# One attention and mixture-of-experts block: scores in one run, a native fp32 weighted sum, and a re-ordered opening

## The chip, the cores and the metric

The kernel runs on one core of one Trainium2 chip. The metric is the device time of one execution in microseconds (us), of which 532.69 is the median of three runs before the change. TensorE (PE in the views) does matmuls and transposes, VectorE (DVE), ScalarE (ACT) and GpSimd (POOL) do element work, and SyncE (SP) issues most of the DMAs. Each engine runs its own instructions in the order of the program and waits on semaphores for the others.

## The reference, cut to what matters

```python
# x: (32, 64, 256); a first layer, then a second one that the change does not touch
xn = ln(x, g_norm)
q = (xn @ Wq).reshape(b, n, 16, 64)          # 16 heads of 64
k, v = split(xn @ Wkv)                       # one key and one value for all heads
k, v = [null_k; k], [null_v; v]              # a null position in front (per batch row)
q, k = l2norm(q) * q_scale, l2norm(k) * k_scale
sim = q @ k.T * 8 + rel_pos_bias(...)        # position network: pos -> ln, silu -> ln, silu -> 16 heads
attn = softmax(where(causal & mask, sim, -big))
z = ln((attn @ v) @ Wout, g_out)
x = x + (((z Wq'.T)(z Wk'.T).T * scale * decay) @ (z Wv'.T)) @ Wo'.T * out_scale
x = x + ffn(moe(x))                          # router, 8 experts, shared expert, dense layer
```

## The kernel before

The 2048 rows are 16 tiles of 128 rows (NT = 16), and a tile is two sequences of 64 rows, b = 0 in the partitions 0 to 63 and b = 1 in 64 to 127. The first layer is a software pipeline over an index i from -2 to 18. In one body(i) the engines work on several tiles at once: the projection of tile i+1, the scores of tile i, the weighted sum of tile i-1, the output projection and second norm of tile i-2, and the retrieval of tile i-3. `live(off)` says whether tile i+off exists. The bodies -2 to 3 and the last ones are written out with extra steps between them, and 4 to 13 are a loop. The order of each engine is the order in which its block is written; nothing plans it.

What a body does, as far as the change touches it:

- Tile i+1: ScalarE makes `xn` from the row statistics, TensorE transposes it into bank 0, ScalarE and VectorE split it into an upper and a lower part (`xnT_h`, `xnT_l`, type fp32r), and TensorE multiplies by the projection in three banks, 384 columns each (`split_passes`, lines 317 to 319: three passes of the split product). An extra matmul with `nvhl` (line 1417) subtracts the null value from v. Squares, sums and a power on GpSimd give `rn`, with which VectorE writes `qn`.
- The value of a tile is laid out as a block diagonal matrix in `vblk_h`, `vblk_l` (four copies on ScalarE, four subtractions on VectorE).
- Tile i: 32 small matmuls (64 rows by 64 columns of the array, 65 columns moved, line 1375) give the scores. The two heads of the last pair share bank 3; TensorE waits for the first (`sc7`) and does the second behind the retrieval's matmuls (line 1388). VectorE adds the bias (`biasm`) in three pieces to `sim`, takes the maximum; GpSimd subtracts it, ScalarE takes the exponential `pe`, VectorE sums (`den`) and inverts (`rden`), and GpSimd writes `pr`.
- Tile i-1: TensorE transposes `pr` (line 1400), ScalarE and VectorE split it into `pT_h` and `pT_l`, and two times three fp32r matmuls over 128 rows, 512 columns each, give the weighted sum in banks 6 and 7. ScalarE and VectorE split that into `oT_h` and `oT_l`.
- Tile i-2: 16 matmuls with `oT_h` and 8 with `oT_l` (line 1339), then the statistics of the second norm.
- The statistics of the rows of x are taken tile by tile: `layer_norm_stats` on VectorE between the sums of the squares, and four small operations on GpSimd behind the `rn` (lines 564 to 570).

The opening (bodies -2 to 0) has beside that the position network (`position_stats`, `hidden_transpose`, `hidden_project`, `silu`), which ends in `relT`, a store to DRAM and two loads back as `bias`; the folding of the retrieval's weights (`fold_qk`, `fold_vo`); and the splitting of the weights, `wout_lower` among them. GpSimd makes the constants (`constants`, `late_constants`) before the first `rn`.

Of the kernel before, what the change touches and what calls it, by code (L numbers as in the profile page):

```python
# [3 lines left out]
F32 = mybir.dt.float32  # L4
# [4 lines left out]
ALU = mybir.AluOpType  # L9
# [38 lines left out]
def adaln_attention_ffn(nc, a, out):  # L48
    ctx = ExitStack()
    with ctx:  # L50
# [39 lines left out]
        with ExitStack() as first:  # L90
# [11 lines left out]
            nvhl = s1('nvhl', [2, DH], F32R)  # L102
            nvf = s1('nvf', [2, DH])
# [8 lines left out]
            ve1 = s1('ve1', [P, 1])  # L112
            ve2 = s1('ve2', [P, 1])
            rs1 = s1('rs1', [P, 1])
            rs2 = s1('rs2', [P, 1])
            nb1 = s1('nb1', [P, 1])
            nb2 = s1('nb2', [P, 1])
            nm1 = s1('nm1', [P, 1])
            nm2 = s1('nm2', [P, 1])
            fixed = s1('fixed', [P, 2])  # L120
            xn = s1('xn', [P, D])
# [10 lines left out]
            vblk_h = s1('vblk_h', [P, 2, 2, P], F32R)  # L132
            vblk_l = s1('vblk_l', [P, 2, 2, P], F32R)
# [13 lines left out]
            with ExitStack() as early2:  # L147
# [11 lines left out]
                nkB, nullb, nvr = nulls[:, 0:DH], nulls[:, DH:DH + H], nulls[0:2, DH + H:2 * DH + H]  # L159
                nksq = s2('nksq', [P, DH])  # L160
                mask_u = s2('mask_u', [P, NT, S], U8)
                zeros = s2('zeros', [P, 2, 2, P])
            pT_h = s1('pT_h', [P, HP, P], F32R)
            pT_l = s1('pT_l', [P, HP, P], F32R)
# [64 lines left out]
        for n in '''ld_x0 ld_x1 ld_x2 ld_rows ld_qkv ld_q2 ld_out ld_att ld_mlp ld_cols ld_mask ld_late st_rel ld_bias ld_u ld_f st_out  # L229
                    pc vc p_const p_tables p_ln    v_zero v_null  v_ln v_hn  # L230
                    v_rawqkv v_lower v_fold   v_decay  v_lin
                    a_sil a_qkvh a_wouth  a_decay   a_tables  
                    t_hT t_mlp t_fold    unit_h unit
                    mv1 ln1_ve ln1_rs ln1_nb xn xnT xnT_h xnT_l qkv sq ss ss_c rn qn kn2 v_h
                    kT_t kh sc7 vblk qT_t qT sim_t biasm sim mx simc pe den rden pr
                    pT_t pT_h pT_l av_t oT_h oT_l wo_t mv2 ln2_ve ln2_rs ln2_nb zn
# [26 lines left out]
        def score_place(r, c):  # L263
            return (bank[3], r * NK) if c == LAST_PAIR else (bank[2 - r], c * NK)

        def score_part(t, m):
            return t[:, 2 * LAST_PAIR:H, :] if m == 2 else t[:, 1 - m:2 * LAST_PAIR:2, :]

        def score_bank(m):
            n = (LAST_PAIR, LAST_PAIR, 2)[m]  # L270
            return bank[1 + m][:, 0:n * NK].rearrange('p (h k) -> p h k', k=NK)
# [43 lines left out]

        def split_passes(e, dst, stat, mov, start, stop, **kw):
# [12 lines left out]
        def _(e):  # L329
# [10 lines left out]
            e.dma_start(nulls[:, :], a['nulls'].to_broadcast([P, 2 * DH + H])).then_inc(sems['ld_cols'], 16)  # L340
# [14 lines left out]
            for b in range(2):  # L355
                e.dma_start(bias[b * S:(b + 1) * S, :, 0:S], rel_dram.ap().rearrange('h i j -> i h j')).then_inc(sems['ld_bias'], 16)
# [61 lines left out]
        def _(e):  # L418
# [21 lines left out]
            def constants():  # L440
                e.memset(zeros[:, :, :, :], 0.0).then_inc(sems['pc'], 1)
                e.wait_ge(sems['pc'], upto('pc'))
# [14 lines left out]
            def late_constants():  # L457
                e.wait_ge(sems['ld_mask'], 16 * 1)
                e.tensor_scalar(mneg[:, :, 0:S], mask_u[:, :, :], -1.0, BIG, ALU.add, ALU.mult).then_inc(sems['pc'], 1)
                e.wait_ge(sems['pc'], upto('pc'))  # L460
                e.memset(zrow[:, :], 0.0).then_inc(sems['pc'], 1)
# [8 lines left out]
                e.wait_ge(sems['pc'], upto('pc'))  # L470
                for n in range(WORD):
# [11 lines left out]

            def after_norm0():
                constants()
                position_norm(1)
# [3 lines left out]
                late_constants()  # L490

            def after_first_projection():
                e.wait_ge(sems['rn'], NB3)
                e.wait_ge(sems['ln1_nb'], 2)
                e.wait_ge(sems['v_null'], 2)
                e.tensor_copy(kh[:, :, S], colsc[:, NKK:NKK + 1].to_broadcast([P, 2])).then_inc(sems['p_tables'], 1)
                e.wait_ge(sems['p_tables'], upto('p_tables'))
                e.tensor_copy(bias[:, :, S:NK], nullb.rearrange('p (h o) -> p h o', o=1)).then_inc(sems['pc'], 1)
                e.wait_ge(sems['pc'], upto('pc'))

            def first_bias():
                e.wait_ge(sems['ld_bias'], 16 * 2)
# [9 lines left out]
            def mask_decay():  # L512
                e.wait_ge(sems['a_decay'], 3)
# [5 lines left out]
            def after_second_scores():  # L519
                e.wait_ge(sems['v_lower'], 1)  # L520

            def mask_bias(i):
                e.wait_ge(sems['sim'], due(NB3 * i))
# [7 lines left out]
            def body(i, par, live, part):  # L531
                if live(0):
                    e.wait_ge(sems['rn'], due(NB3 * (i + 1)))
                    e.wait_ge(sems['ln1_nb'], due(i + 2 if live(1) else NT))
# [27 lines left out]
                if live(2):  # L562
                    e.wait_ge(sems['mv1'], due(2 * (i + 3)))
                    e.tensor_tensor(nm1[:, :], mv[:, 0, 0:1], fixed[:, 1:2], ALU.mult)
                    e.tensor_tensor(ve1[:, :], mv[:, 0, 1:2], fixed[:, 0:1], ALU.add).then_inc(sems['ln1_ve'], 1)
                    e.wait_ge(sems['ln1_ve'], due(i + 3))
                    e.wait_ge(sems['xn'], due(i + 2))
                    e.tensor_tensor(rs1[:, :], ve1[:, :], half[:, 0:1], ALU.pow).then_inc(sems['ln1_rs'], 1)
                    e.wait_ge(sems['ln1_rs'], due(i + 3))
# [1134 lines left out]
```

## Time and profile before

| what | value |
|---|---|
| time, median of 3 runs (lowest, highest) | 532.69 us (531.86, 539.52) |
| span of the profiled execution | 532.0 us |
| TensorE busy | 468.7 us (88%) |
| VectorE, ScalarE, GpSimd busy | 359.7, 274.7, 284.7 us |
| mean granted clock of TensorE | 0.958 |

The profiled execution's own time is its span, 532.0 us, which is 0.7 us under the median; the views below are all of that execution. The span is read in three stretches: the opening to about 60 us, the tiles of the first layer to about 295 us, and the second layer behind it. Busy shares are means over all three.

### The profile page before, as it was taken

Reading aid. Unit: us, or ns where it says so; the run is one execution under the profiler, and the core shown is the slowest. Engines: PE = TensorE matmul, PEld = TensorE weight load, DVE = VectorE, ACT = ScalarE, POOL = GpSimd, SP = SyncE. Lnnn points to the kernel's source line nnn. Section 1 sums busy time; section 2 is a strip of 40 time slices with the busy share of each in tenths; the row PEclk is TensorE's granted clock in tenths of the full one; section 3 lists DMA queues with packets and bytes.
Section 4 is the critical chain, followed back from the end, with each engine's and each line's share of the span. In section 5 each row is a group of like instructions: output and inputs, shape, how many; then the busy total and the mean of one; then the engine's idle time right before and its main releaser. Section 6 shows DMA issues by size and latency. Waiting matters only on the chain.

```text
span 532.0 us, 11898 instructions
## 1 busy us (share of the span) xinstructions
PE 468.7 (88%) x3961; PEld 418.7 (79%) x3961; DVE 359.7 (68%) x879; ACT 274.7 (52%) x574; POOL 284.7 (54%) x343
## 2 busy tenths in 40 slices
PE   3946889999999999999999896499989489999997
PEld 1735777898999988898888785398989359898986
DVE  4784888888889888898766475757664524444522
ACT  3426666576667666566652422246565234453442
POOL 3738778897987979797830777400000633425100
PEclk9966999999999999999998998989999879999999
DMA  8370103709082641000010323265752312213011
GB/s 263 90 192 1 31 1 111 257 26 343 0 292 72 208 157 30 0 30 1 1 31 2 99 100 108 82 206 185 235 169 100 89 33 57 80 41 96 25 41 39
DMA packets 51616, 52.17 MB, mean 98 GB/s; under 512 B 6645, under 2 KB 49015, under 8 KB 51577
## 3 DMA queue, kind: packets, MB, share of 16 engines
q1 hardware_dynamic: 47956, 42.98, 25.5%
q0 software_dynamic: 3072, 8.39, 5.0%
q8 instruction: 23, 0.38, 0.3%
q10 hardware_dynamic: 548, 0.28, 0.2%
q14 instruction: 17, 0.13, 0.1%
HBM read 22.03 MB, written 29.62 MB: 97 GB/s over the span
## 4 chain that ended last, share of the span: by engine, by line
PE 59%; issue 8%; POOL 8%; ACT 5%; DMA 3%; DVE 3%; SPq 1%; DVEq 0%; ACTq 0%; POOLq 0%
PE bank L317 10%; PE bank L318 9%; PE bank L319 9%; POOL slot_x L579 6%; PE bank L322 5%; PE bank L323 5%; PE bank L1375 3%; PE bank L1655 3%; PE bank L1400 2%; PE bank L1339 2%; PE bank L1443 2%; ACT qT L666 2%; PE bank L1351 1%; PE bank L1388 1%; DMA slot_y<-yb 1%
## 5 line engine op out<-in xcount | busy, mean ns | idle before, releaser
L588 POOL DMA_INDIRECT yg<-slot_y,yrow x32 | 34.2, 1068 | 120.8 <-DMA slot_y<-yb 76.3
L561 POOL TENSOR_TENSOR rn<-sc,half 128x6 f32<-128x6 f32 (+1 forms) x48 | 60.6, 1277 | 7.9 <-DVE sc L1023 6.9
L1256 DVE TENSOR_TENSOR hl<-hw,hh 128x512 fp32r<-128x512 f32 x32 | 22.2, 693 | 57.1 <-ACT hw L837 57.1
L835 ACT ACTIVATE hh<-bank,late 128x512 fp32r<-128x512 f32 x32 | 22.0, 688 | 53.5 <-PE bank L1655 41.9
L317 PE MATMUL bank<-wqkv_h,xnT_h 128*128 128x384 f32 x96 | 39.1, 408 | 6.8 <-DVE sim L1004 6.8
L556 POOL TENSOR_TENSOR sim<-sim,mx 128x1040 f32<-128x1040 f32 x16 | 31.3, 1955 | 23.0 <-DVE mx L1007 23.0
L695 ACT ACTIVATE sq<-bank 128x384 f32<-128x384 f32 (+1 forms) x48 | 22.8, 475 | 40.3 <-PE bank L319 24.7
L524 POOL TENSOR_TENSOR biasm<-bias,mneg 128x1040 f32<-128x1040 f32 x16 | 35.7, 2229 | 3.7 <-DMA bias<-rel_scratch 3.7
L579 POOL DMA_INDIRECT slot_x<-xs,posi x32 | 31.4, 980 | 11.2 <-issue 9.4
L542 POOL TENSOR_TENSOR pr<-pe,rden 128x1024 f32<-128x1024 f32 x16 | 30.4, 1903 | 9.2 <-DVE rden L1044 4.5
L322 PE MATMUL bank<-wout_h,oT_h 128*128 128x256 f32 x128 | 33.6, 296 | 1.9 <-DVE oT_l L1038 1.9
L318 PE MATMUL bank<-wqkv_l,xnT_h 128*128 128x384 f32 x96 | 34.5, 359 | 0.0
L319 PE MATMUL bank<-wqkv_h,xnT_l 128*128 128x384 f32 x96 | 34.3, 358 | 0.0
L322 PE MATMUL bank<-w_h,hh 128*128 128x256 f32 x128 | 32.5, 287 | 0.0
L323 PE MATMUL bank<-wout_l,oT_h 128*128 128x256 f32 x128 | 32.4, 289 | 0.0
L323 PE MATMUL bank<-w_l,hh 128*128 128x256 f32 x128 | 32.0, 283 | 0.0
L1020 DVE TENSOR_REDUCE ss<-sq 128x6 f32<-128x384 f32 (+1 forms) x48 | 25.2, 526 | 7.5 <-ACT sq L695 7.4
L1004 DVE TENSOR_TENSOR sim<-bank,biasm 128x455 f32<-128x455 f32 (+1 forms) x48 | 21.9, 513 | 11.2 <-PE bank L1375 11.2
L674 ACT ACTIVATE zn<-bank,nb,rs 128x256 f32<-128x256 f32 x16 | 9.1, 566 | 39.4 <-POOL nb L551 39.4
L317 PE MATMUL bank<-wu_h,bxT_h 128*128 x80 | 25.1, 314 | 2.5 <-DVE bxT_l L1205 2.5
L322 PEld LDWEIGHTS bank<-wout_h,oT_h 128*128 128x128 f32 x128 | 24.9, 195 | 2.5 <-issue 1.4
L317 PEld LDWEIGHTS bank<-wqkv_h,xnT_h 128*128 128x128 f32 x96 | 19.5, 204 | 9.1 <-issue 8.3
(317 smaller groups left out, 1604.8 us busy)
## 6 DMA issues: line engine op xcount, KB each, us to landing
slot_x<-zrow SPq DMA_DIRECT2D x4, 4352.0 KB, 14.4
xq<-slot_x SPq DMA_DIRECT2D x40, 128.0 KB, 2.1
slot_y<-yb SPq DMA_DIRECT2D x20, 256.0 KB, 2.4
fstage<-in_f_W SPq DMA_DIRECT2D x4, 512.0 KB, 4.5
out<-p_all SPq DMA_DIRECT2D x8, 256.0 KB, 2.1
xs<-in_x SPq DMA_DIRECT2D x1, 1536.0 KB, 9.5
raw_out<-in_c_Wout SPq DMA_DIRECT2D x1, 1024.0 KB, 7.8
stage<-in_m_wgate SPq DMA_DIRECT2D x8, 128.0 KB, 2.1
```

Of the source, the lines that this page charges most:

```text
L317: e.matmul(dst, stat[0], mov[0], start=start, stop=False, **kw)
L318: e.matmul(dst, stat[0], mov[1], start=False, stop=False, **kw)
L319: return e.matmul(dst, stat[1], mov[0], start=False, stop=stop, **kw)
L322: e.matmul(dst, stationary, moving[0], start=start, stop=False, **kw)
L323: e.matmul(dst, stationary, moving[1], start=False, stop=False, **kw)
L524: e.tensor_tensor(biasm[:, :, :], bias[:, :, :], (mneg[:, i:i + 1, :] if isinstance(i, int) else mneg[:, bass.ds(i, 1), :]).to_broadcast([ ...
L542: e.tensor_tensor(pr[:, :].rearrange('p (h k) -> p h k', h=H), pe[:, :, 0:S], rden[:, :].rearrange('p (h o) -> p h o', o=1).to_broadcast([ ...
L556: e.tensor_tensor(sim[:, :, :], sim[:, :, :], mx[:, :].rearrange('p (h o) -> p h o', o=1).to_broadcast([P, H, NK]), ALU.subtract).then_inc ...
L561: e.tensor_tensor(rn[:, lo:hi], sc[:, lo:hi], half[:, lo:hi], ALU.pow).then_inc(sems['rn'], 1)
L579: e.indirect_dma_start(out=xdram.ap()[:, :], out_offset=bass.IndirectOffsetOnAxis(ap=posi[:, t, r:r + 1], axis=0), in_=xs[:, t, :], in_off ...
L588: e.indirect_dma_start(out=yg[:, g % 2, r, t, :], out_offset=None, in_=ydram.ap()[:, :], in_offset=bass.IndirectOffsetOnAxis(ap=yrow[:, g ...
L1020: e.reduce_sum(ss[:, lo:hi], sq[:, lo:hi, :], AX_X).then_inc(sems['ss'], 1)
```

## The change

- **Scores.** The two sequences of a tile take opposite row halves of the array: for b = 1 the heads of a pair are exchanged (`r ^ b`), in the scores, in the null bias and in the loads of `bias`. The last pair goes to banks 3 and 5, so the wait `sc7` goes, and the 32 matmuls stand in one run. The bias is added in four pieces instead of three.
- **Weighted sum.** `pT_h`, `pT_l`, `vblk_h`, `vblk_l` and `nvhl` go. There is one fp32 copy `pT` and two values `v_own` and `v_other` (three subtractions of `nvB` on VectorE, at the end of the body), and the sum is four fp32 matmuls over 64 rows and 64 columns of the array, 512 columns moved.
- **Order in a body.** On TensorE the eight matmuls with `oT_l` stand behind the transposes of `qn`. On VectorE `qn` stands ahead of `den` and `rden`. On ScalarE `kn2` stands ahead of `oT_h` and `pe`.
- **Row statistics.** They are taken in groups of tiles, X_GROUPS = (0), (1), (2, 3), (4 to 7), (8 to 11), (12 to 15): `row_stats` at the end of VectorE's bodies -1 to 3 and `norm_rows` behind GpSimd's.
- **Opening.** `hidden_project(0)` stands ahead of the transposes of `xn`, `position_scale(0)` ahead of the wait for the small tables; ScalarE loads its function tables early by two one-column activations (`warm`); `late_constants` is cut in three, of which two stand behind the first projection's `rn`; `wout_lower` moves from body 0 to behind body -1, `fold_vo` from ahead of the scores' bias to behind the maximum.

```diff
+        X_GROUPS = ((0, 1), (1, 2), (2, 4), (4, 8), (8, 12), (12, NT))
+        SCORES = ((2 * LAST_PAIR, H - 1, 3), (2 * LAST_PAIR + 1, H, 5), (1, 2 * LAST_PAIR, 1), (0, 2 * LAST_PAIR, 2))
...
             def after_first_projection():
                 e.wait_ge(sems['rn'], NB3)
-                e.wait_ge(sems['ln1_nb'], 2)
                 e.wait_ge(sems['v_null'], 2)
                 e.tensor_copy(kh[:, :, S], colsc[:, NKK:NKK + 1].to_broadcast([P, 2])).then_inc(sems['p_tables'], 1)
                 e.wait_ge(sems['p_tables'], upto('p_tables'))
+                norm_rows(1)
                 e.tensor_copy(bias[:, :, S:NK], nullb.rearrange('p (h o) -> p h o', o=1)).then_inc(sems['pc'], 1)
                 e.wait_ge(sems['pc'], upto('pc'))
+                row_constants()
+                late_constants()
...
+            def norm_rows(n):
+                t0, t1 = X_GROUPS[n]
+                e.wait_ge(sems['mvx'], 2 * (n + 1))
+                e.tensor_tensor(nmx[:, t0:t1], mvx[:, t0:t1, 0], fixed[:, 1:2].to_broadcast([P, t1 - t0]), ALU.mult)
...
+                e.tensor_tensor(rsx[:, t0:t1], vex[:, t0:t1], half[:, 0:t1 - t0], ALU.pow).then_inc(sems['ln1_rs'], 1)
...
             def after_first_scores():
+                norm_rows(2)
...
             def after_second_scores():
+                norm_rows(3)
                 e.wait_ge(sems['v_lower'], 1)
...
-                    e.wait_ge(sems['ln1_nb'], due(i + 2))
+                    e.wait_ge(sems['ln1_nb'], x_groups_for(i + 1 if isinstance(i, int) else i))
...
+            def row_stats(n):
+                t0, t1 = X_GROUPS[n]
+                e.wait_ge(sems[('ld_x0', 'ld_x0', 'ld_x1', 'ld_x2', 'ld_x2', 'ld_x2')[n]], 16 * 1)
+                for t in range(t0, t1):
+                    last = e.bn_stats(stx[:, t - t0, :], xs[:, t, :])
...
+                if live(1):
+                    e.wait_ge(sems['av_t'], due(2 * i))
...
+                    e.tensor_tensor(v_own[:, 1 - par, :], bank[NB3][:, values], nvB[:, :], ALU.subtract)
...
+                if isinstance(i, int) and FIRST_I < i < FIRST_I + len(X_GROUPS):
+                    row_stats(i - FIRST_I)
...
-                    head = slice(r * DH, (r + 1) * DH)
                     for b in range(2):
+                        head = slice((r ^ b) * DH, ((r ^ b) + 1) * DH)
                         last = e.matmul(dst[b * S:(b + 1) * S, lo:lo + NK], qT[head, c, b * S:(b + 1) * S], kh[head, b, :], start=True, stop=True)
...
-                        last = split_passes(e, bank[6 + b][:, :], (vblk_h[:, 1 - par, b, :], vblk_l[:, 1 - par, b, :]), (pT_h[:, :, b * S:(b + 1) * S], pT_l[:, :, b * S:(b + 1) * S]), True, True)
...
+                    for q in range(2):
+                        rows = slice(q * S, (q + 1) * S)
+                        for b in range(2):
+                            r = q ^ b
+                            value = (v_other if r else v_own)[rows, 1 - par, :]
+                            last = e.matmul(bank[6 + b][r * DH:(r + 1) * DH, :], value, pT[rows, :, b * S:(b + 1) * S], start=True, stop=True)
```

TensorE's order in the second half of the loop's body, before: from the last matmuls with `oT_l` to the transposes of `pr`.

```order
L1339 MATMUL bank<-wout_h,oT_l 128x256 x8
L1344 MATMUL bank<-ident,kn 128x128
L1348 REGISTER_ALU
L1351 MATMUL bank<-ident,qn 128x128 x4
L1348 REGISTER_ALU
L1351 MATMUL bank<-ident,qn 128x128 x4
L1354 REGISTER_ALU
L1357 MATMUL bank<-ident,xn 128x128 x2
L1363 MATMUL bank<-uT,znT 128x128
L1367 REGISTER_ALU
L1369 MATMUL bank<-uT,znT 128x128
L1375 MATMUL bank<-kh,qT 64x65 x30
```

The same place after the change. The matmuls with `oT_l` (now line 1374) stand between the transposes of `qn` and of `xn`, and all 32 scores (now line 1398) stand in one run ahead of the retrieval (line 1411).

```order
L1369 MATMUL bank<-ident,qn 128x128 x4
L1374 MATMUL bank<-wout_h,oT_l 128x256 x8
L1377 REGISTER_ALU
L1380 MATMUL bank<-ident,xn 128x128 x2
L1386 MATMUL bank<-uT,znT 128x128
L1390 REGISTER_ALU
L1392 MATMUL bank<-uT,znT 128x128
L1398 MATMUL bank<-kh,qT 64x65 x32
L1411 MATMUL bank<-at,zn 128x128 x2
```

GpSimd's order from the last `rn` of body 1 to `pr` of body 2, before. `nm`, `ve`, `rs`, `nb` are the row statistics of one tile, made of what VectorE left between its sums.

```order
L561 TENSOR_TENSOR rn<-sc,half 128x6 x2
L564 TENSOR_TENSOR nm<-mv,fixed 128x1
L565 TENSOR_TENSOR ve<-mv,fixed 128x1
L568 TENSOR_TENSOR rs<-ve,half 128x1
L570 TENSOR_TENSOR nb<-nm,rs 128x1
L524 TENSOR_TENSOR biasm<-bias,mneg 128x1040
L542 TENSOR_TENSOR pr<-pe,rden 128x1024
```

The same place after. The four operations are now of a group of four tiles and stand between `biasm` and `pr`.

```order
L594 TENSOR_TENSOR rn<-sc,half 128x6 x2
L558 TENSOR_TENSOR biasm<-bias,mneg 128x1040
L505 TENSOR_TENSOR nmx<-mvx,fixed 128x4
L506 TENSOR_TENSOR vex<-mvx,fixed 128x4
L508 TENSOR_TENSOR rsx<-vex,half 128x4
L510 TENSOR_TENSOR nbx<-nmx,rsx 128x4
L575 TENSOR_TENSOR pr<-pe,rden 128x1024
```

VectorE's order at the end of body 0 after the change: the statistics that `norm_rows(2)` waits for come behind `qn`, `den`, `rden` and the values.

```order
L1057 TENSOR_TENSOR qn<-bank,rn 128x384 x2
L1063 TENSOR_REDUCE den<-pe 128x16
L1066 RECIPROCAL rden<-den 128x16
L1072 TENSOR_TENSOR v_own<-bank,nvB 128x64
L1075 TENSOR_TENSOR v_other<-bank,nvB 64x64 x2
L991 BN_STATS stx<-xs 128x6 x2
L254 MEMSET carrier 128x1
L996 BN_AGGR mvx<-stx 128x2 x2
L1013 TENSOR_TENSOR xnT_l<-bank,xnT_h 128x256
```

Before, that place reads as follows, without statistics: they stand further up, between the sums of the squares.

```order
L1041 TENSOR_REDUCE den<-pe 128x16
L1044 RECIPROCAL rden<-den 128x16
L1055 TENSOR_TENSOR qn<-bank,rn 128x256
L1055 TENSOR_TENSOR qn<-bank,rn 128x384 x2
L986 TENSOR_TENSOR vblk_l<-bank,vblk_h 64x64
L986 TENSOR_TENSOR vblk_l<-bank,vblk_h 64x64 x3
L993 TENSOR_TENSOR xnT_l<-bank,xnT_h 128x256
```

## Rows read from the trace of the kernel before

**Rows 1.** The page's first line.
```profile
span 532.0 us, 11898 instructions
```

**Rows 2.** Timeline of TensorE, one tile: start, us, instruction [idle before].
```profile
186.82 0.39 PE L1363 MATMUL bank<-uT,znT 128*128 128x128 f32 x2
187.48 0.49 PE L1369 MATMUL bank<-uT,znT 128*128 128x128 f32 x2 [0.27 <-ACT qT L666]
187.90 1.15 PE L1375 MATMUL bank<-kh,qT 64*64 64x65 f32 x60
188.98 0.71 PE L1388 MATMUL bank<-at,zn 128*128 128x128 f32 x4
189.62 0.33 PE L1375 MATMUL bank<-kh,qT 64*64 64x65 f32 x4
189.88 1.10 PE L1400 MATMUL bank<-ident,pr 128*128 128x128 f32 x8
...
191.69 0.33 PE L319 MATMUL bank<-wqkv_h,xnT_l 128*128 128x384 f32 x1
...
192.18 0.44 PE L317 MATMUL bank<-wqkv_h,xnT_h 128*128 128x384 f32 x1
...
194.61 0.39 PE L317 MATMUL bank<-pT_h,vblk_h 128*128 128x512 f32 x1
...
196.00 0.28 PE L317 MATMUL bank<-wvo_h,rT_h 128*128 128x256 f32 x1
...
196.72 1.06 PE L1443 MATMUL bank<-znT,mqk 128*128 128x128 f32 x8
197.54 0.36 PE L322 MATMUL bank<-wout_h,oT_h 128*128 128x256 f32 x1
...
204.78 1.09 PE L1400 MATMUL bank<-ident,pr 128*128 128x128 f32 x8
```

**Rows 3.** Timeline of VectorE in the same tile.
```profile
193.73 0.43 DVE L974 BATCH_NORM_STATS2 st<-xs 128x6 f32 x1
...
194.30 0.55 DVE L1020 TENSOR_REDUCE ss<-sq 128x6 f32<-128x384 f32 x1
...
197.88 1.24 DVE L1041 TENSOR_REDUCE den<-pe 128x16 f32<-128x1040 f32 x1 [0.18 <-ACT pe L708]
199.15 0.25 DVE L1044 RECIPROCAL rden<-den 128x16 f32<-128x16 f32 x1
...
200.87 0.92 DVE L986 TENSOR_TENSOR vblk_l<-bank,vblk_h 64x64 fp32r<-64x64 f32 x4
```

**Rows 4.** Timeline of GpSimd in the same tile.
```profile
193.86 3.90 POOL L561 TENSOR_TENSOR rn<-sc,half 128x5 f32<-128x5 f32 x3 [0.20 <-DVE sc L1023]
...
198.13 0.55 POOL L568 TENSOR_TENSOR rs<-ve,half 128x1 f32<-128x1 f32 x1
...
198.90 2.24 POOL L524 TENSOR_TENSOR biasm<-bias,mneg 128x1040 f32<-128x1040 f32 x1
201.43 1.90 POOL L542 TENSOR_TENSOR pr<-pe,rden 128x1024 f32<-128x1024 f32 x1 [0.29 <-POOL biasm L524]
```

**Rows 5.** Timeline of the opening, GpSimd.
```profile
18.33 0.31 POOL L461 MEMSET zrow<- 128x256 f32 x1
...
22.55 3.77 POOL L561 TENSOR_TENSOR rn<-sc,half 128x5 f32<-128x5 f32 x3
...
31.82 2.19 POOL L524 TENSOR_TENSOR biasm<-bias,mneg 128x1040 f32<-128x1040 f32 x1 [3.70 <-DMA bias<-rel_scratch]
```

**Rows 6.** Timeline of the opening, VectorE and then TensorE.
```profile
31.87 4.30 DVE L938 TENSOR_TENSOR wout_l<-raw_out,wout_h 128x2048 fp32r<-128x2048 f32 x1
...
37.71 0.66 PE L317 MATMUL bank<-wqkv_h,xnT_h 128*128 128x384 f32 x1 [5.76 <-DVE sim L1004]
...
52.19 1.89 PE L1375 MATMUL bank<-kh,qT 64*64 64x65 f32 x64 [0.35 <-ACT qT L666]
```

**Rows 7.** Busy time in one stretch: TensorE busy, granted clock, DMA.
```profile
46.00:48.00 2.00, 0.00 (x0) 0.74 0.00 0
```

More of the change, by code:

```diff
@@ L512, in mask_decay @@
             def mask_decay():
+                norm_rows(4)
                 e.wait_ge(sems['a_decay'], 3)
@@ L977, in layer_norm_stats @@
                 settle(e)
-                e.bn_aggr(mv[:, n, :], st6[:, n, :]).then_inc(sems[m], 1)
+                for t in range(t0, t1):
+                    last = e.bn_aggr(mvx[:, t, :], stx[:, t - t0, :])
+                last.then_inc(sems['mvx'], 1)
+                e.wait_ge(sems['mvx'], 2 * n + 2)
             def body(i, par, live, part):
+                if isinstance(i, int) and i == FIRST_I:
+                    row_stats(0)
                 at_step(after_xn, i)
-                if live(0):
-                    e.wait_ge(sems['v_h'], due(i + 1))
-                    for b, r in ((0, 0), (0, 1), (1, 0), (1, 1)):
-                        at_b = (slice(r * DH, (r + 1) * DH), par, b, slice(r * DH, (r + 1) * DH))
-                        last = e.tensor_tensor(vblk_l[at_b], bank[NB3][b * S:(b + 1) * S, QB - DH:QB], vblk_h[at_b].bitcast(F32), ALU.subtract)
-                    last.then_inc(sems['vblk'], 1)
@@ L1336, in body @@
                         upper_passes(e, bank[6][:, 0:D], (wout_h[:, c, :], wout_l[:, c, :]), oT_h[:, c, :], c == 0)
-                    e.wait_ge(sems['oT_l'], due(2 * (i - 1)))
-                    for c in range(HP):
-                        last = e.matmul(bank[6][:, 0:D], oT_l[:, c, :], wout_h[:, c, :], start=False, stop=c == HP - 1)
-                    last.then_inc(sems['wo_t'], 1)
                 if live(0):
@@ L1352, in body @@
                         last.then_inc(sems['qT_t'], 1)
+                if live(-2):
+                    e.wait_ge(sems['oT_l'], due(2 * (i - 1)))
+                    for c in range(HP):
+                        last = e.matmul(bank[6][:, 0:D], oT_l[:, c, :], wout_h[:, c, :], start=False, stop=c == HP - 1)
+                    last.then_inc(sems['wo_t'], 1)
                 if live(1):
@@ L1397, in body @@
                     for c in range(2):
+                        if c == 1 and live(0):
+                            e.wait_ge(sems['sim'], due(NS4 * i + 2))
                         for j in range(4):
@@ L1411, in body @@
                     for m, c in enumerate(BANKS3):
-                        e.wait_ge(sems['sim'], due(NB3 * (i + 1)))
+                        e.wait_ge(sems['sim'], due(NS4 * (i + 1)))
                         at_step(before_bank[m], i)
+                        if m == NB3 - 1 and live(-1):
+                            before_av()
                         for k in range(KD):
                             last = split_passes(e, bank[1 + c][:, 0:QB], (xnT_h[:, k, :], xnT_l[:, k, :]), (wqkv_h[:, k, c * QB:(c + 1) * QB], wqkv_l[:, k, c * QB:(c + 1) * QB]), k == 0, k == KD - 1)
-                        if c == NB3 - 1:
-                            last = e.matmul(bank[NB3][:, QB - DH:QB], ones[0:2, :], nvhl[:, :], start=False, stop=True, skip_group_check=True)
                         last.then_inc(sems['qkv'], 1)
```

244 lines of the change are left out of this document (120 added, 124 removed).

## The prediction

> **What bounds the kernel now.** I read the span first [rows 1], then TensorE's timeline in a tile of the first layer [rows 2], then the same tile on VectorE and GpSimd [rows 3, 4], then the opening [rows 5 to 7]. The transposes of `pr` begin at 189.88 and again at 204.78: a tile costs 14.90 us. TensorE issues nearly without a gap in it; its only idle time is 0.27 us ahead of line 1369, for ScalarE's copy of `qT` [rows 2]. So in the steady tiles any time taken from TensorE's list shortens the tile, as long as the others keep up. The opening is bound otherwise. TensorE sits idle for 5.76 us until 37.71, since the bias addition (`sim`) waits for `biasm` (31.82 + 2.19 = 34.01) and then for VectorE, which is in `wout_l` from 31.87 for 4.30 us [rows 5, 6]. The second layer is not touched and only shifts.
>
> **The change, steady tiles.** All terms are start to start on TensorE.
>
> *Weighted sum.* The six fp32r matmuls take 194.61 to 196.00, 1.39 us, or 0.232 each [rows 2]. The new ones are fp32; the trace records a normal fp32 matmul twice, and the eight records of line 1443 (four matmuls) take 0.82 us, 0.103 for 128 columns, so 0.41 for 512 [rows 2]. Four matmuls are eight records: 3.3 us if they run one behind the other. The scores show that they need not: they are fp32 in the same quarter-array shape, their 65 columns would be 0.052 by that rate, and 60 of them go in 1.08 us, 0.018 each, 2.9 at once [rows 2]. At 2.9 at once the sum is 1.14 us, at four 0.82. Entering the shape costs about 0.2: the pair of line 1369 takes 0.42 to the first score, a pair at 0.103 each would be 0.21 [rows 2]. So 1.0 to 1.35; I take 1.2, nearest to the scores' rate. Saved: 0.2.
>
> The Trainium skill ("TensorEngine Tiling (Array Packing)", Key Properties) says that a change of tiling mode drains TensorE; the 0.2 above agrees, and it leaves little of the gain.
>
> *The `nvhl` matmul.* 191.69 to 192.18 is 0.49 where two passes of 384 columns follow each other, by the rate of the 512-column passes 0.17 [rows 2]. Saved: 0.3.
>
> *The wait for `qT`.* 186.82 to 187.48 is 0.66 where a pair needs 0.21 [rows 2]. The eight matmuls with `oT_l` now stand in that place and cover the copy. Saved: 0.45. If the cover were gone it would come back whole.
>
> *Scores in one run.* The last four records cost 0.26, as part of a run 0.07 [rows 2]. Saved: 0.2.
>
> Against that, both halves of the weighted sum now end together, so the split into `oT_h` and `oT_l` starts later; I count 0.05. In all 1.1 us a tile: 13.8 instead of 14.9. The other engines allow it: GpSimd loses the four row operations, VectorE loses `pT_l`, `vblk_l` and its row statistics and gains three small subtractions, and ScalarE loses four copies. Tiles with this gain are those of bodies 2 to 14, and the last ones have about 1.5 more: 13 x 1.1 + 1.5 = 16 us.
>
> **The change, row statistics.** This is where I expect the gain to go. `norm_rows` stands ahead of `pr` on GpSimd and waits for `row_stats`, which stands at the very end of VectorE's body, behind `qn`, `den`, `rden` and the values. Behind the waiting GpSimd are queued `pr` and the next subtraction of the maximum; TensorE waits for `pr` ahead of its transposes and then of the next projection. Counted from the end of `rden`, at which `pr` could start: the values, 3 x 0.23 = 0.7 (`vblk_l`, 0.92 for four); four tiles of statistics, at most 4 x 0.57 = 2.3 (193.73 to 194.30 for one), at least 4 x 0.43 = 1.7 (the first operation alone), taken as 2.2 [rows 3]; four operations on GpSimd, 1.14 for one column (the `rn` end at 197.76, `biasm` begins at 198.90), and the power over four columns between 0.55 (one) and 1.30 (six), taken as 1.0, so 1.6 [rows 4]. Together 4.5, with bounds 3.6 and 4.9.
>
> What slack is there? `rden` ends at 199.40 now and will end 1.7 later, behind `qn` and one addition: 201.1, with `pr` to 203.0. The transposes of `pr` would come at 204.78 less 0.65 (the `qT` wait and the run of scores): 204.1 [rows 2 to 4]. Slack 1.1, so a stall of 3.4 in a full body. In body 2 the retrieval's matmuls are not there yet and the slack is 0.2: 4.3. In body 3 GpSimd has the decay's selection besides: 3.9; in body 4 3.4. Some 11.5 us in three bodies; about 1.5 of it falls on waits that these bodies have now (two function-table loads of ScalarE stand there in both kernels). Net loss 10 us, bounds 7 and 12.
>
> **The change, opening.** The position network ends about 1.8 us earlier by the chain of its steps, so `bias` could be there at 30. But 4.2 us of constants, which ran from 18.33 to 22.55 while GpSimd had nothing to do, now stand behind `norm_rows(1)`, which waits for statistics at the end of VectorE's body -1, about 27. Constants end near 32.5, `biasm` near 34.7. `wout_l` no longer stands ahead of `sim`, so the addition starts at 34.8, the next projection near 36.4 instead of 37.71 [rows 5, 6]: 1.3 gained. Then `xn` of tile 2 is the first instruction of ScalarE's body 1, with the copies of `kh` and `qT` queued behind it, and it waits for `norm_rows(2)`, hence for `den`, `rden`, the values and two tiles of statistics: about 50.8, which puts the scores near 52.9 where they are at 52.19 [rows 6]. The table load of the exponential (hidden now by `warm`) and `qn` ahead of `den` gain nothing, since this chain ends last. I count +1.5 at tile 2, bounds -1.5 and +3, part of it the clock.
>
> **Clock.** With TensorE idle the granted clock falls to 0.74 in the mean of 46 to 48 us, that is from the level of 2.4 GHz to 1.2 GHz within it [rows 7]. The new stalls are about as long as that one. Each fall would cost 2 to 3 us of passes at half speed; I count 2 in all, bounds 0 and 8.
>
> **Sum.** 532.0 - 16 + 10 + 1.5 + 2 = 529.5, about 530 us; against the median of 532.69 it would be 530.2. The bounds of the terms give 520 to 541.
>
> **Rivals.**
>
> *The statistics are covered.* If VectorE reaches them earlier than I count, or GpSimd is late anyway, no stall appears in bodies 2 to 4 and the opening gains its 1 to 2 us: 532 - 16 - 1.5 = 514.5. For it: VectorE loses over 2 us of work a tile. Against it: the statistics stand behind `den`, which waits for ScalarE, and ahead of them nothing is loose.
>
> *The four fp32 matmuls do not overlap.* Both row halves of the array now write into one bank at once, in the scores and in the weighted sum; before, every run keeps them in different banks, and the last pair is kept apart by a wait, so no row shows what it costs. If they take turns in pairs, the sum is 1.65 + 0.2 and the scores cost 1.1 more, 1.75 us a tile, 24 us over 14 tiles: 554. It decides from a sum of about 2.0 us a tile on. The Trainium skill (same page, Restrictions and Gotchas) says that different row tiles cannot access the same PSUM bank at the same time; whether partitions that differ lift that, no row shows. Wholly in series the sum alone costs 2.1 more than my 1.2, over 16 tiles 34 us: 564.
>
> *The clock falls in every stall.* The forecast with 8 instead of 2 and the upper bounds of the stalls: 540 to 545.
>
> **Chances.** The forecast 0.65; statistics covered 0.15; no overlap, in pairs or in series 0.11; clock 0.09. A measurement of this kernel tells about 2% (10.7 us) from no change. Faster by more than that, under 522.0, is the covered case and a little of the forecast's lower end: 0.20. Slower, over 543.3: 0.14. Within: 0.66. The range leaves out the overlap case and part of the first: 514 to 543.
>
> **What the profile after would show.** Right: a steady tile of 13.7 to 13.9 us, no idle time ahead of line 1392, a waiting `pr` and 3 to 4 us of idle TensorE ahead of the transposes of `pr` in each of bodies 2, 3 and 4, `biasm` of tile 0 beginning when the constants end, not when the load lands, and `xn` of tile 2 waiting for GpSimd. Wrong: a weighted sum of over 1.5 us; `pr` that starts right behind `rden` in body 2; a steady tile that another engine sets, GpSimd first, which in a tile with `wu_l` has over 13 us of work.

## The result

The changed kernel takes 534.48 us (median of 20 runs, 532.32 to 541.96) where the kernel before takes 532.74 (20 runs, 530.3 to 540.69). The ratio is 1.004, with a 95% interval of 1.0021 to 1.0058: it is slower by a little, within the 2% called the same, and not faster by 0.5% as forecast. Some runs are 1 to 2% longer at a lower granted clock, and each ratio here leaves those out, so it need not be the quotient of the two medians. Both profiled executions have a span of 532.0 us [rows 1], so in them what the change gives and what it takes cancel. The page of the kernel after begins:

```profile
span 532.0 us, 11720 instructions
...
PE 458.2 (86%) x3977; PEld 403.4 (76%) x3977; DVE 340.7 (64%) x832; ACT 258.7 (49%) x512; POOL 276.6 (52%) x302
```

TensorE has 10.5 us less to do (468.7 before) and is as late at the end, so it stands idle 10.5 us more. Its timeline in a steady tile (start, us, instruction), to be read against [rows 2]:

```profile
183.57 1.04 PE L1423 MATMUL bank<-ident,pr 128*128 128x128 f32 x8
184.37 0.45 PE L330 MATMUL bank<-wqkv_h,xnT_h 128*128 128x384 f32 x1
...
187.70 0.33 PE L332 MATMUL bank<-wqkv_h,xnT_l 128*128 128x384 f32 x1
187.96 0.64 PE L1460 MATMUL bank<-pT,v_own 64*64 64x512 f32 x1
187.97 0.65 PE L1460 MATMUL bank<-pT,v_other 64*64 64x512 f32 x2
187.98 1.05 PE L1460 MATMUL bank<-pT,v_own 64*64 64x512 f32 x2
188.45 0.60 PE L1460 MATMUL bank<-pT,v_other 64*64 64x512 f32 x2
188.46 0.59 PE L1460 MATMUL bank<-pT,v_own 64*64 64x512 f32 x1
188.98 0.38 PE L330 MATMUL bank<-wvo_h,rT_h 128*128 128x256 f32 x1
...
189.79 1.05 PE L1474 MATMUL bank<-znT,mqk 128*128 128x128 f32 x8
190.94 0.39 PE L335 MATMUL bank<-wout_h,oT_h 128*128 128x256 f32 x1
...
195.35 0.48 PE L1392 MATMUL bank<-uT,znT 128*128 128x128 f32 x2
195.76 1.16 PE L1398 MATMUL bank<-kh,qT 64*64 64x65 f32 x64
196.85 0.71 PE L1411 MATMUL bank<-at,zn 128*128 128x128 f32 x4
197.40 1.04 PE L1423 MATMUL bank<-ident,pr 128*128 128x128 f32 x8
```

From one row of transposes of `pr` to the next are 13.83 us, 14.90 before. Now the waits of TensorE from 60 to 300 us (us in total, times, the longest):

```profile
PE bank L1380 <- ACT kh L691: 5.2, 2, 5.0
PE bank L1423 <- POOL pr L575: 5.0, 2, 4.1
PE bank L1411 <- DVE at L1018: 3.8, 4, 1.5
PE bank L335 <- DVE oT_l L1049: 3.3, 4, 1.7
```

The first two lie in bodies 3 and 4 and in bodies 2 and 3; of the third 1.5 us lie in body 3 and 2.3 in the last bodies, where the kernel before has 2.2. The fourth is mostly ahead of bodies 2, 3 and 4. This is the timeline there: TensorE, VectorE and GpSimd in body 2, TensorE in body 3, then TensorE, GpSimd and ScalarE in body 4:

```profile
67.85 1.16 PE L1398 MATMUL bank<-kh,qT 64*64 64x65 f32 x64
73.06 1.97 PE L1423 MATMUL bank<-ident,pr 128*128 128x128 f32 x8 [4.05 <-POOL pr L575]
66.59 0.25 DVE L1066 RECIPROCAL rden<-den 128x16 f32<-128x16 f32 x1
...
67.42 1.41 DVE L991 BATCH_NORM_STATS2 stx<-xs 128x6 f32<-128x256 f32 x4
...
69.33 0.20 POOL L505 TENSOR_TENSOR nmx<-mvx,fixed 128x4 f32<-128x4 f32 x1 [2.92 <-DVE mvx L996]
...
71.11 1.90 POOL L575 TENSOR_TENSOR pr<-pe,rden 128x1024 f32<-128x1024 f32 x1
...
91.25 0.71 PE L1411 MATMUL bank<-at,zn 128*128 128x128 f32 x4 [1.49 <-DVE at L1018]
92.95 1.09 PE L1423 MATMUL bank<-ident,pr 128*128 128x128 f32 x8 [0.99 <-POOL pr L575]
...
103.85 1.19 PE L1374 MATMUL bank<-wout_h,oT_l 128*128 128x256 f32 x8
110.06 0.66 PE L1380 MATMUL bank<-ident,xn 128*128 128x128 f32 x2 [5.02 <-ACT kh L691]
...
107.07 0.20 POOL L505 TENSOR_TENSOR nmx<-mvx,fixed 128x4 f32<-128x4 f32 x1 [3.16 <-DVE mvx L996]
...
108.59 0.20 POOL L510 TENSOR_TENSOR nbx<-nmx,rsx 128x4 f32<-128x4 f32 x1
...
109.06 0.60 ACT L688 ACTIVATE xn<-xs,nbx,rsx 128x256 f32 x1 [7.13 <-POOL nbx L510]
109.57 0.35 ACT L691 ACTIVATE kh<-bank,colsc 128x128 f32<-128x128 f32 x1
```

In body 2 it is as forecast: `pr` starts 4.27 us behind the end of `rden` (66.84), and TensorE is idle for 4.05. In body 4 something else ends last. `xn` on ScalarE waits 7.13 us for `nbx` of the last group, whose statistics reach GpSimd at 107.07, and the copy of `kh`, which TensorE needs, is queued behind it. Behind both stalls TensorE's work is slow. The stretches, with TensorE busy, granted clock and DMA:

```profile
70.00:80.00 10.00, 6.94 (x32) 0.66 0.00 0
...
110.00:120.00 10.00, 9.94 (x110) 0.72 0.16 54
```

0.66 and 0.72 are means between the levels of 1.2 and 2.4 GHz; both stretches had 1.00 before. The eight records of transposes take 1.97 us instead of 1.04.

A body of TensorE begins with its first matmul with `oT_h` (line 335, 322 before). From one start to the next, in us:

| | start of body 2 | body 2 | body 3 | body 4 | bodies 5 to 13, mean | start of 14 |
|---|---|---|---|---|---|---|
| before | 61.86 | 15.26 | 16.12 | 14.90 | 14.90 | 242.24 |
| after | 63.64 | 18.98 | 18.34 | 21.26 | 13.74 | 245.92 |

The first layer's last transposes of `xs` begin at 301.27 (300.84 before). So the account is: opening +1.78, bodies 2 to 4 +12.30, bodies 5 to 13 -10.40, body 14 and the end -3.25, in all +0.43 us; behind that the second layer is as much shorter. The opening differs between executions: in six further ones that do not differ from the changed kernel up to there (e1, e5, e7, e8, e11 and e12) body 2 starts between 63.50 and 65.65. So the accounts of two single executions show where the gain went, and not the 0.4% by which the medians differ.

### The profile page after: what moved, and what is told of

Read it like the earlier page. It is cut to its first block, busy times and chain, and to the rows that moved or that the text cites. A ratio compares the mean times of both kernels' runs of the same rounds, so it can differ in the third digit from the quotient of the medians.

```text
span 532.0 us, 11720 instructions
## 1 busy us (share of the span) xinstructions
PE 458.2 (86%) x3977; PEld 403.4 (76%) x3977; DVE 340.7 (64%) x832; ACT 258.7 (49%) x512; POOL 276.6 (52%) x302
## 4 chain that ended last, share of the span: by engine, by line
PE 43%; POOL 21%; issue 14%; DVE 12%; ACT 5%; DMA 3%; SPq 1%; POOLq 0%; DVEq 0%; ACTq 0%
PE bank L330 7%; PE bank L331 6%; PE bank L332 6%; POOL slot_x L603 6%; PE bank L335 4%; PE bank L336 4%; PE bank L1686 3%; POOL sim L589 3%; POOL pr L575 2%; DVE den L1063 2%; POOL rn L594 2%; DVE qn L1057 2%; ACT oT_h L736 2%; PE bank L1423 2%; PE bank L1398 2%
## 5 line engine op out<-in xcount | busy, mean ns | idle before, releaser
L330 PE MATMUL bank<-wqkv_h,xnT_h 128*128 128x384 f32 x96 | 38.0, 396 | 7.0 <-DVE sim L1024 4.2
L603 POOL DMA_INDIRECT slot_x<-xs,posi x32 | 31.4, 980 | 11.2 <-issue 9.5
L1049 DVE SCALAR_TENSOR_TENSOR oT_l<-bank,colsc,oT_h 128x512 fp32r<-128x512 f32 x32 | 22.5, 746 | 13.8 <-ACT oT_h L736 13.8
L1024 DVE TENSOR_TENSOR sim<-bank,biasm 128x65 f32<-128x65 f32 (+1 forms) x64 | 24.1, 422 | 9.7 <-PE bank L1398 5.5
```

What stands on the lines that cost most here:

```text
L603: e.indirect_dma_start(out=xdram.ap()[:, :], out_offset=bass.IndirectOffsetOnAxis(ap=posi[:, t, r:r + 1], axis=0), in_=xs[:, t, :], in_off ...
```

## The experiments

Each ratio is to the kernel before on the same chip; its median there was 547.08 us for e1 to e4, 547.26 for e5 to e8, 537.06 for e9 and e10, 533.17 for e11 and e12, so that only ratios are compared across these groups; e1 to e8 have nearly the same base, and for them the difference from e5 is given in us too. Unless said otherwise an experiment is an edit of the changed kernel.

**e5: the base.** No edit.

> The changed kernel once more, unaltered, beside the kernel before on the chip of these runs, as the base for the other three. Expected: 1.004 of the kernel before, as in the first comparison, with an interval of about 0.2%.

548.19 us, 1.0027 (1.0006 to 1.0047). The small loss is there on a second chip. Bodies 2 to 4: 18.19, 18.34, 21.30. In body 2 the same operations wait on each other, but TensorE sits idle for only 2.52 us, since it is late itself: from 65.65 to 69 its matmuls with `oT_h` are 0.43 us apart and not 0.24. What is longer on this chip lies behind the first layer: 244.1 us from the last transposes of `xs` to the end, 230.7 in the first profile.

**e3: statistics tile by tile.**

```diff
+                if live(2) and not (isinstance(i, int) and i == FIRST_I):   # VectorE, behind sums(0)
+                    e.bn_stats(stx[:, 0, :], at_tile(xs, i + 2)).then_inc(sems['mvx'], 1)
...
-                if isinstance(i, int) and FIRST_I < i < FIRST_I + len(X_GROUPS):
-                    row_stats(i - FIRST_I)
...
-                norm_rows(1)   # and 2, 3, 4, 5; GpSimd's four operations stand behind rn in each body
```

> The changed kernel with the row statistics undone alone: each tile's statistics again in the body before, ahead of the second sums on VectorE and behind the rn powers on GpSimd, for one tile a body; only tile 0 keeps its own. Theory (grouping and its place cost 16 us in bodies 2 to 4 and 1.5 to 3 us at tile 2): 534.5 - 16 - 2 = 516.5, less what a steady tile gives back where GpSimd has 1.14 us more (its list would be about 13.0 us, 13.9 in a tile with wu_l, where TensorE's is 13.74): 0 to 3 us, so 516 to 520. Rival (the loss comes from the rest of the change, the new order of the opening above all): 528 or more.

533.56 us, 0.9758 (0.9732 to 0.9784): 2.7% or 14.6 us less than e5. Bodies 2 to 4 take 15.58, 15.54 and 13.80. Body 2 begins at 57.19 instead of 63.64, more than I had expected: `norm_rows(1)` no longer holds the constants, so `biasm` begins at 29.74 instead of 32.48, and `xn` of tile 2 begins at 45.13 instead of 51.79, right behind its own statistics. Of the 20.1 us that it is ahead at the start of body 5 the steady tiles give 4.9 back (102.11 to 230.76 is 14.29 a tile). The loss of the change is its statistics.

**e1: the loop from body 6.**

```diff
-        STEADY0, STEADY1 = (4, NT - 3)
+        STEADY0, STEADY1 = (6, NT - 3)
```

> The changed kernel with the rolled loop beginning at body 6 instead of body 4, so that bodies 4 and 5 know their number and ScalarE's normalization of the row tiles 5 and 6 waits for their own group of statistics, not for all six groups. Nothing else is changed. Theory (the third stall, 5.0 us of idle TensorE in body 4 and about 2.5 us of work at the 1.2 GHz level behind it, is this wait for the last group): the transposes of the normalized tile run at about 105 in body 4, and the wait moves to the transposes of the probabilities, which begin near 111.1 where they are at 114.6 now: 3.5 us less, 531.0 against 534.5. Rival (the third stall is GpSimd's late product of probabilities, as I forecast): no change within 0.5 us.

544.92 us, 0.9963 (0.9936 to 0.999): 3.3 us less than e5. Body 4 takes 16.94 us instead of 21.26. TensorE's waits in it are now these:

```profile
108.79 0.71 PE L1411 MATMUL bank<-at,zn 128*128 128x128 f32 x4 [1.34 <-DVE at L1018]
111.29 1.09 PE L1423 MATMUL bank<-ident,pr 128*128 128x128 f32 x8 [1.79 <-POOL pr L575]
```

Two short waits, with the clock up, take the place of one of 5.02 with slow work behind it. The third stall of the changed kernel is the wait for all six groups.

**e11 and e12: GpSimd's operations behind `pr`.**

```diff
                     e.tensor_tensor(pr[:, :]..., ALU.mult).then_inc(sems['pr'], 1)
+                if isinstance(i, int) and 2 <= i <= 3:     # e12: 2 <= i <= 4, and the loop from body 6
+                    norm_rows(i + 1)
...
-                norm_rows(3)   # and 4; e12: and 5
```

> The changed kernel with GpSimd's four row operations of bodies 2 and 3 moved from ahead of the product of probabilities to behind it; VectorE's statistics stay at the end of the bodies before, and body 4 is as it is. It splits the stall of a body into GpSimd's queue and VectorE's. Theory (TensorE then waits in body 2 for VectorE's additions, which come behind the statistics, from 69.0 to about 70.9 instead of for the probabilities until 73.06, and in body 3 the selection on the decay no longer waits either): 2.2 us less idle time and most of the 2.3 us of half-speed work in body 2, 1.5 to 2 us in body 3, 4 to 6 us or 0.75 to 1.1% less than the changed kernel, a ratio to the kernel before of 0.993 to 0.996. Rival (VectorE's place alone holds TensorE, GpSimd's queue is hidden behind it): under 1 us gained, 1.001 or more.

> The run before and the one with the rolled loop from body 6 together, with the row operations of body 4 behind the product of probabilities too, so that in bodies 2, 3 and 4 neither GpSimd's product nor ScalarE's normalization waits for statistics, while VectorE still does them at the end of bodies 1, 2 and 3. Theory: what is left is VectorE's part alone, the four tiles of statistics (1.9 us a body with their aggregation) ahead of the additions: the three bodies take about 14.9 + 1.9 us or less each, 8 to 11 us less than the changed kernel, a ratio of 0.983 to 0.988. Rival (the waits move to another operation of GpSimd or ScalarE): 0.992 or more.

e11: 529.02 us, 0.9885 (0.9844 to 0.9927). e12: 525.71 us, 0.981 (0.9744 to 0.9876), from six runs. By the traces bodies 2 to 4 are 6.2 us shorter than in the first profile in e11 (15.39, 15.83, 21.21), where I had expected 4 to 6, and 12.2 in e12 (15.39, 15.93, 15.06), where I had expected 8 to 11. The ratio of e11 is better than I had expected too; the interval of e12 reaches into the expected range. What is left of the stall of body 2 in e11 is VectorE's part:

```profile
71.73 1.06 PE L1423 MATMUL bank<-ident,pr 128*128 128x128 f32 x8 [1.38 <-DVE xnT_l L1013]
```

It is 1.38 us instead of 4.05, and the granted clock stays at 1.00 from 70 to 80. So most of the loss is in the queues: operations that wait for statistics stand ahead of others that don't need them, on GpSimd and then on ScalarE.

**e2: statistics earlier on VectorE.** `row_stats(3)` to `(5)` move from the end of a body to behind its maximum.

```diff
-                if isinstance(i, int) and FIRST_I < i < FIRST_I + len(X_GROUPS):
+                if isinstance(i, int) and FIRST_I < i < 1:
                     row_stats(i - FIRST_I)
...
+                if isinstance(i, int) and 1 <= i < FIRST_I + len(X_GROUPS):   # ahead of the sums
+                    row_stats(i - FIRST_I)
```

> The changed kernel with the statistics of the last three groups (four tiles each) moved on VectorE from the end of bodies 1, 2 and 3 to behind the maximum of the same bodies, where VectorE waits for ScalarE's squares; GpSimd's order is as it is. Theory (bodies 2, 3 and 4 lose 11.6 us of idle TensorE and about 4.8 us of half-speed work because GpSimd and ScalarE wait for statistics that stand last on VectorE): the three stalls go, VectorE's delay of body 1 costs about 0.7 back, 534.5 - 15 = 519.5, range 517 to 523. Rival (the statistics cost by being VectorE work, not by their place): the sums and qn come later instead, and under 4 us are gained, 530 or more.

535.73 us, 0.9818 (0.9783 to 0.9854): 12.5 us less than e5 by the medians, 11.4 by the ratios, and by the traces the first layer ends 11.2 us earlier (291.43 against 302.59). The theory's range began at 11.5, so it is met at its lower edge at best. The bodies are level at 16.00, 16.04 and 15.99. TensorE no longer waits for `pr`, but for `oT_l` (2.41, 2.02 and 0.82 us), and in body 4 still for `kh`:

```profile
102.48 0.41 PE L1382 MATMUL bank<-ident,xn 128*128 128x128 f32 x2 [1.84 <-ACT kh L691]
```

`xn` waits there for the last group, for 3.95 us, as in the changed kernel; only the group is ready earlier. The rival is right for about 2 us in each of bodies 2 and 3.

**e8: the wait filled.**

```diff
+                    if isinstance(i, int) and i == 2:
+                        for j in range(32):
+                            e.transpose(bank[4][:, j % 4 * P:(j % 4 + 1) * P], ident[:, :], ident[:, :])
                     e.wait_ge(sems['pr'], due(i))
```

> The changed kernel with 32 more transposes of the identity on TensorE in body 2, into a bank that is free there, ahead of its wait for the product of probabilities; their result is not used. They take about 3.6 us of the 4.05 us in which TensorE is idle there. Theory (the stall costs twice, once as idle time and once because the work behind it runs at the 1.2 GHz level from 73.06 to about 78): the granted clock stays at 1.00 from 70 to 80, the transposes of the probabilities take 1.09 instead of 1.97 us, and the next weighted sum comes 2.3 us earlier; 0.4% less than the changed kernel. Rival (the slow passes have another cause): no change, or the added work is added to the time.

547.23 us, 1.0004 (0.9988 to 1.0021), 1.0 us under e5; the intervals overlap, so the whole time shows no gain. The added transposes, and a stretch with the clock kept up:

```profile
71.64 3.68 PE L1419 MATMUL bank<-ident 128*128 128x128 f32 x32 [1.36 <-DVE xnT_l L1013]
...
70.00:80.00 10.00, 8.63 (x85) 1.00 0.01 2
```

The added work runs until 75.3 and so outlasts `pr`, which is ready at 74.25: the transposes of `pr` begin at 75.16, 0.9 us later than they could, and take 1.04 us. From them to the weighted sum are 4.35 us (75.16 to 79.51), 6.74 in the first profile (73.06 to 79.80), so the slow rows cost 2.4 us there. Bodies 2 to 4 together take 56.82 us, 58.58 in the first profile; e5, with 57.83, has its slow rows elsewhere. Body 2 is 1.5 us shorter than in the first profile, which is the 2.4 less the 0.9 of the added work; body 3 is 0.7 longer and body 4 0.9 shorter. What the fall of the clock costs at the end is not resolved: the bodies say 1 to 1.8 us, and the whole time 1.0 with overlapping intervals.

**e7: the cover of the `qT` copy taken away.** The eight matmuls with `oT_l` go back ahead of the transposes of `kn` and `qn`.

> The changed kernel with the eight matmuls that take oT_l moved back ahead of the transposes of kn and qn on TensorE, as in the kernel before; nothing else is changed. Theory (they hide ScalarE's copies of kh and qT): a steady tile goes from 13.74 to 14.2 us, and over fourteen tiles the time rises by 5 to 6.5 us, 1.0 to 1.2% over the changed kernel. Rival (the copies are not on the path once GpSimd and VectorE have less to do): no change within 1 us.

551.99 us, 1.0096 (1.0069 to 1.0123): 3.8 us more than e5. TensorE waits for `qT` again, 12 times from 60 to 300 us, and bodies 5 to 13 take 14.01 us instead of 13.74 ((248.12 - 122.02) / 9). The cover is worth 0.27 us a tile and not 0.45: without it the stretch ahead of line 335 is shorter (191.11 to 192.02 against 189.79 to 190.94), so that 0.24 us of what the cover gives is lost there.

**e6: statistics in pairs.** One pair of tiles in every second body, at e3's places, and `row_constants` ahead of the second position norm.

> The changed kernel with the row statistics in pairs of tiles, in every second body: on VectorE behind the first sums, on GpSimd behind the rn powers, tiles 0 and 1 at the start, none of them ahead of the product of probabilities; and with the constants of the row tables (five operations, 1.6 us) moved ahead of the second position norm. Theory: no stall is left in bodies 2 to 4, GpSimd has 1.3 us per two tiles in place of the 2.3 of the run with one tile a body, so that a steady tile is set by TensorE again at 13.8 us, and tile 1 no longer waits in the opening: 20 us less than the changed kernel, a ratio to the kernel before of 0.966, range 0.962 to 0.972. Rival (something else than the statistics and GpSimd holds the tiles of the run with one tile a body): 0.975 as there.

534.58 us, 0.9792 (0.9763 to 0.9822): the theory fell. The bodies alternate between 15.05 and 13.59; the long ones are those in whose time GpSimd does the pair. In the changed kernel the same bodies take 13.84, so that GpSimd operations of 1.3 us in all cost 1.2. Their number of elements is not what costs, their place is: behind `rn` and ahead of `biasm` and `pr`, where GpSimd has 0.2 us of idle time left.

**e9: statistics where time is idle.** On VectorE one tile a body ahead of the sums (tile i + 4), on GpSimd a pair ahead of the wait for the maximum in the bodies without `wu_l`.

```diff
                     e.tensor_tensor(nb2[:, :], nm2[:, :], rs2[:, :], ALU.mult).then_inc(sems['ln2_nb'], 1)
...
+                if live(2) and par == 0 and not (isinstance(i, int) and i == FIRST_I):
+                    norm_pair(i, part[0] + 1)
                 if live(0):
                     e.wait_ge(sems['mx'], due(i + 1))
```

> The changed kernel with the row statistics put where the traces show idle time: on VectorE one tile a body ahead of the first sums, two to four bodies before they are needed, and on GpSimd a pair of tiles in every second body ahead of its wait for the maximum, in those bodies where it has no wu_l to do and is idle for 1.58 us there; the constants of the row tables ahead of the second position norm as in the run in pairs. Bodies 12 and 13 are written out in place of the last passes of the loop. Theory (GpSimd in the bodies with the added operations is what made 15.05 us of a 13.6 us body in the run in pairs, 1.3 us of operations and nothing to hide them): every steady tile is at 13.6 to 13.9 us, and the ratio to the kernel before is 0.967, range 0.963 to 0.971. Rival (VectorE's statistics, 0.43 us a tile, are what lengthens the body): 14.2 us a tile and 0.975 or more.

516.46 us, 0.9706 (0.9643 to 0.977), from six runs: the lowest ratio of all, though its interval overlaps that of e3, and at the upper end of the theory's range. By the traces its first layer ends earliest too (283.25; 287.01 in e6, 287.72 in e3). Bodies 2 to 4 take 14.35, 16.10 and 13.74, and from 5 on they alternate between 13.83 and 13.58, as in the changed kernel, with all the statistics in them. This version beats both kernels.

**e4: constants earlier.** `row_constants()` and `late_constants()` move ahead of `position_norm(1)`.

> The changed kernel with GpSimd's constants (fourteen memsets, iotas and a selection, 4.2 us in the trace from 28.24 to 32.4) moved into the 4.3 us in which GpSimd waits for the second position norm, from 8.75 on. Theory (they hold back the masked bias of tile 0): it starts when the bias load lands, at about 28.5 instead of 32.48, the first projection follows at about 32.8 instead of 36.28, and the whole kernel is 3.5 us shorter: 531.0. Rival (the load lands no earlier than 32): no change within 0.5 us.

545.41 us, 0.9971 (0.9954 to 0.9989), 2.8 us under e5. `biasm` now starts at 29.52, 0.26 us of it waiting for the load, and the projection at 34.49 instead of 36.28. The added operations do not delay the position norm, which starts at 13.05 (13.04 in the first profile). The first profile is not the right thing to set beside it, though. In the executions with this opening unchanged, the first operation of `norm_rows(1)` starts anywhere between 24.70 and 26.89 and `biasm` between 32.40 and 34.61. TensorE is where they part: the pass at 17.35 takes 0.44 us in the first profile, and at 17.81 0.69 in e4 and at 17.82 in e8, at the lower level of the clock. In e4 that operation starts at 25.84; e8 is next to it with 25.56, `biasm` at 33.25 and the projection at 37.05. Against e8 the projection is 2.6 us earlier, close to the gain of the whole.

**e10: `wout_l` later.** `wout_lower()` moves from the end of VectorE's body -1 to the end of body 0.

> The changed kernel with VectorE's subtraction that makes wout_l (2048 elements a row, both operands in SBUF, 2.29 us) moved from the end of body -1 to the end of body 0, where VectorE is idle; nothing else is changed. Theory (GpSimd makes no progress while it runs: its multiplication of one element a row took 2.23 us from 24.76 to 26.99, 0.2 elsewhere, and wout_l ran from 24.65 to 26.94): the multiplication takes 0.2 us, the constants and the masked bias behind it come 2.0 us earlier, and the whole kernel is 2 us or 0.37% shorter than the changed kernel, 0.999 of the kernel before. Rival (the long multiplication is a late start or a wait that the trace does not name): its length stays at 2.2 us and nothing is gained.

534.26 us, 1.0045 (0.999 to 1.01), no gain. The timeline of GpSimd, then VectorE, shows why:

```profile
25.57 0.19 POOL L505 TENSOR_TENSOR nmx<-mvx,fixed 128x1 f32<-128x1 f32 x1 [3.12 <-DVE mvx L996]
...
31.23 2.19 POOL L558 TENSOR_TENSOR biasm<-bias,mneg 128x1040 f32<-128x1040 f32 x1
...
49.04 2.30 POOL L505 TENSOR_TENSOR nmx<-mvx,fixed 128x2 f32<-128x2 f32 x1 [1.55 <-DVE mvx L996]
...
49.00 2.29 DVE L952 TENSOR_TENSOR wout_l<-raw_out,wout_h 128x2048 fp32r<-128x2048 f32 x1
```

The multiplication at 25.57 is short now, as the theory says, and `biasm` starts 2.0 us earlier than in e8 (33.25), where the multiplication starts at the same time (25.56). But `wout_l` came to stand beside the next group's, at 49.04, which is as long instead, and on which `xn` of tile 2 waits: the scores of tile 1 begin at 54.60, and at 54.51 in e8.

## Why the prediction was wrong

The number 530 lies 0.8% under the median, inside the range and inside the 2%; the sign is wrong. Step by step:

- **Steady tiles: right.** 1.16 us a tile against 1.1, -13.65 us from body 5 on against -12.5. The parts were less good than the sum. In the tile shown, the stretch with the `nvhl` matmul gives 0.29 (184.37 to 187.96 against 3.88), the weighted sum 0.37 (1.02 us, at the lower bound), the stretch from the last matmul with `oT_h` to the scores 0.44 (192.93 to 195.76 against 3.27) and the scores 0.34; but from the end of the sum to line 335 it is 1.96 us where it was 1.54, 0.42 lost where I had counted 0.05.
- **No overlap of the fp32 matmuls: refuted.** Four matmuls of 512 columns take 1.02 us, and both row halves write banks 6 and 7.
- **Opening: right, the size in part by luck.** +1.78 against +1.5, where the six other executions would give +1.6 to +3.8 against the one trace of before; `biasm` at 32.48 (forecast 32.5), the projection at 36.28 (36.4), the scores of tile 1 at 53.76 (52.9).
- **Row statistics: right in body 2, in body 3 right in size only.** The stall of body 2 is 4.05 us where 4.3 stood. In body 3 I had forecast 3 to 4 us of idle time ahead of the transposes of `pr`; it is 0.99 there, behind 1.49 for `at`, whose `decay` GpSimd selects behind the same wait. The body is 2.22 us longer than before, 2.3 by my terms, and in e11, without the wait, 2.5 us shorter than here.
- **Row statistics, body 4: the step that failed.** I wrote that "behind the waiting GpSimd are queued `pr` and the next subtraction of the maximum", 3.4 us. I did not follow the other side that waits for `norm_rows`: ScalarE's `xn`, with the copies of `kh` and `qT` behind it. In bodies written out it waits for its own group. In the loop the number of the body is in a register, and `x_groups_for` returns all six groups; body 4 is the first of the loop, and the sixth group is done just then. It costs 5.02 us of idle time at once, and body 4 is 6.36 us longer than before where my terms gave 1.8. e1 takes 4.3 us of that away, and leaves 16.94, with 3.1 us of waits in it, close to the 13.8 + 3.4 of the forecast.
- **Clock: mis-sized.** I counted 2 in all. The slow rows behind the stall of body 2 add up to 2.4 us, those behind that of body 4 to about 2.5. What of the first reaches the end e8 leaves between 1 and 1.8 us, and for body 4 it is not priced apart from the stall. The clock rival's 540 to 545 is not what its terms add up to either: 532 - 16 + 12 + 3 + 8 is 539.

For bodies 2 to 4 my terms, with the clock, came to +8.7 us (-3.3 + 10 + 2), and the traces show +12.30. These 3.6 us, nearly all of them in body 4, less the 0.9 that the rest gave beyond its terms (1.15 in the tiles, less 0.28 in the opening), are what turned -2.3 into +0.43.

## What to carry to other kernels

Batching small work saves instructions, but an operation that waits for a batch holds everything queued behind it; for each one go through every engine that waits for its result, and what each has queued, not only the one that you fear. A wait in a rolled loop has to hold for every pass, so ask what it asks of the first. Before an operation is placed, look in the trace for where that engine is idle: the same 1.3 us cost 1.2 in one place (e6) and nothing in another (e9). And before a difference of 1 or 2 us between two traces is explained, look how far two executions of the same kernel lie apart at that place.

## What the runs showed of the hardware

The changed kernel, GpSimd and then VectorE:

```profile
24.76 2.23 POOL L505 TENSOR_TENSOR nmx<-mvx,fixed 128x1 f32<-128x1 f32 x1 [2.98 <-DVE mvx L996]
...
24.65 2.29 DVE L952 TENSOR_TENSOR wout_l<-raw_out,wout_h 128x2048 fp32r<-128x2048 f32 x1
```

A small GpSimd operation that reads SBUF while VectorE subtracts two SBUF operands of 2048 elements lasts until that ends. It took 2.23 us in the changed kernel (24.76 to 26.99, `wout_l` from 24.65 to 26.94) and 2.30 in e10, 0.19 otherwise. Memsets are not held: in e3, with `wout_l` from 24.38 to 26.67, three on GpSimd take 0.2 to 0.3 us each, and the selection behind them, which reads, takes 1.90 instead of 0.29. Before the change it went the other way round: `biasm` was first, and `wout_l` took 4.30 us [rows 5, 6] where it now takes 2.29. The Trainium skill ("SBUF — State Buffer", SBUF: two separate sides) says that the two engines share a port pair as an exclusive lock for a whole instruction, whichever starts first; these rows agree, with 2.0 to 2.1 us lost where it is the multiplication or `wout_l` that waits.

Four fp32 matmuls on quarters of the array run at once although two row halves write the same PSUM bank, in different partitions: 1.02 us (187.96 to 188.98), where one behind the other would be 3.3 by the rate of the fp32 matmuls in [rows 2]. The Trainium skill ("TensorEngine Tiling (Array Packing)", Restrictions and Gotchas) says that different row tiles can't access the same bank at the same time; this trace does not show such a cost, and the measurement decides.
